# One branch around the whole second layer of a two-layer transformer kernel, six PSUM banks in turn in its feed-forward part, and gathers and modulations issued at other places

## The reference

```python
# attention: 16 heads, 64 anchors
anchor_B = qk @ W_anchor.T * SCALE
attn = softmax(anchor_B, axis=-1)
s = sum(attn, axis=-2); recip = 1 / s
out = einsum('bhna,bhnd->bhad', attn, v)
out = recip[..., None] * out
out = einsum('bhna,bhad->bhnd', attn, out)
out = out @ W_out.T + b_out
# feed-forward: width 512
h = silu(x @ w1.T * s1) * (x @ w2.T * s2)
h = gelu(h @ h1.T * sh1); h = gelu(h @ h2.T * sh2)
y = h @ w3.T * s3
# around both: layernorm, times (1 + c), plus s; result times a gate, plus x
```

## Time and profile before

| | |
|---|---|
| median of 3 runs | 864.3 us (861.33 to 867.69) |
| the profiled execution: its time / its span | 871.6 us / 869.8 us |
| busy share: PE, DVE, ACT, POOL | 80%, 64%, 48%, 32% |
| mean granted clock of PE | 0.885 of full |
| the chain that ended last: PE, DVE, POOL, issue, DMA, ACT | 53%, 16%, 13%, 8%, 4%, 4% |
| first tile's sum of batches 0, 1, 2, 3 starts at (L553) | 380.36, 505.33, 628.88, 752.17 us |

### The profile page before, as it was taken

The page is one execution under the profiler, slowest core; times in us unless marked ns, Lnnn a source line. Parts: engine busy times, 40 slices in busy tenths (PEclk is TensorE's granted clock), DMA queues, the critical chain, the costliest instruction groups (busy, mean ns, idle before and its releaser), DMA issues.

```text
span 869.8 us, 9514 instructions
## 1 busy us (share of the span) xinstructions
PE 700.2 (80%) x3009; PEld 498.2 (57%) x3009; DVE 559.6 (64%) x1355; ACT 416.9 (48%) x701; POOL 279.9 (32%) x222
## 2 busy tenths in 40 slices
PE   3676555379999992099888989979898989899997
PEld 1665444358888881055546845546655458555465
DVE  4585554747677671558487579586586875676563
ACT  2455332257777770134337534347444265343474
POOL 2347787600000003627531047430058230043000
PEclk8788755579999997569899999999999999799999
DMA  5244337727677661000000000000000000000000
GB/s 202 109 146 172 140 123 271 274 61 252 237 236 266 228 211 61 24 1 24 25 0 1 1 32 25 19 2 0 26 16 26 9 1 1 26 1 1 0 1 26
DMA packets 21554, 71.22 MB, mean 82 GB/s; under 512 B 4908, under 2 KB 5172, under 8 KB 17080
## 3 DMA queue, kind: packets, MB, share of 16 engines
q1 hardware_dynamic: 17400, 62.08, 20.3%
q0 software_dynamic: 4096, 8.40, 3.2%
HBM read 47.38 MB, written 23.08 MB: 81 GB/s over the span
## 4 chain that ended last, share of the span: by engine, by line
PE 53%; DVE 16%; POOL 13%; issue 8%; DMA 4%; ACT 4%; another core or an unknown queue 1%; SPq 0%; DVEq 0%; ACTq 0%; POOLq 0%
PE ps L1389 13%; PE ps L1385 7%; PE ps L1391 7%; POOL rows_by_expert L498 7%; PE ps L1393 6%; PE ps L1392 6%; PE ps L1645 5%; POOL yb L525 3%; DVE hid L1283 2%; PE ps L1633 2%; DMA wbuf<-w_split 2%; DVE stats L894 2%; PE ps L1661 2%; DVE ring L1299 2%; POOL misc L563 2%
## 5 line engine op out<-in xcount | busy, mean ns | idle before, releaser
L525 POOL DMA_INDIRECT yb<-y_by_expert,ypos x64 | 64.0, 1000 | 184.2 <-DMA y_by_expert<-ysb 168.0
L1389 PE MATMUL ps<-hid,fh 128*128 128x512 f32 x256 | 103.6, 405 | 6.6 <-DVE hid L1283 4.9
L1391 PE MATMUL ps<-hid,fh 128*128 128x512 f32 x256 | 100.3, 392 | 0.0
L563 POOL TENSOR_TENSOR misc<-misc,ring 128x1024 f32<-128x1024 f32 x28 | 65.9, 2354 | 51.6 <-DVE ring L1273 38.1
L498 POOL DMA_INDIRECT rows_by_expert<-h,pos x64 | 68.4, 1069 | 23.1 <-issue 19.8
L1283 DVE TENSOR_TENSOR hid<-ring,hid 128x512 fp32r<-128x512 f32 x56 | 45.1, 810 | 46.5 <-ACT hid L794 45.2
L1389 PEld LDWEIGHTS ps<-hid,fh 128*128 128x128 f32 x256 | 48.1, 188 | 25.9 <-DVE hid L1283 11.3
L1645 PE MATMUL ps<-ring,hn 128*128 128x512 f32 x112 | 55.5, 618 | 5.3 <-DVE ring L1273 5.3
L1177 DVE TENSOR_TENSOR hid<-ring,hid 128x512 fp32r<-128x512 f32 x46 | 31.8, 692 | 41.9 <-ACT hid L590 41.9
L1661 PE MATMUL ps<-attnT,cmat 128*128 128x512 f32 x128 | 56.9, 592 | 0.0
L1252 DVE TENSOR_REDUCE nmax<-ps 128x16 f32<-128x1024 f32 x32 | 39.2, 1224 | 25.5 <-PE ps L1393 25.5
(11 more groups left out here) (278 smaller groups left out, 1744.8 us busy)
## 6 DMA issues: line engine op xcount, KB each, us to landing
wbuf<-w_split SPq DMA_DIRECT2D x23, 1024.0 KB, 5.3
w_split<-parts SPq DMA_DIRECT2D x4, 2048.0 KB, 7.6
xs<-rows_by_expert SPq DMA_DIRECT2D x23, 256.0 KB, 5.3
y_by_expert<-ysb SPq DMA_DIRECT2D x23, 256.0 KB, 5.6
raw<-in_w SPq DMA_DIRECT2D x8, 512.0 KB, 8.4
ffn_raw<-in_ffn SPq DMA_DIRECT2D x1, 2816.0 KB
rows_by_expert<-zeros SPq DMA_DIRECT2D x9, 256.0 KB, 8.2
xa<-in_x SPq DMA_DIRECT2D x4, 512.0 KB, 6.0
```

The lines of the kernel that those rows point to most:

```text
L525: gp.indirect_dma_start(yb[:, k, t, :], None, ydisp, bass.IndirectOffsetOnAxis(ypos[:, b, k, t:t + 1].bitcast(U32), 0))\
L563: gp.tensor_tensor(asum, asum, ring[:, 2 * (t % 2):2 * (t % 2) + 2, :] .rearrange("p a n -> p (a n)"), ALU.add).then_inc(*pool_asum.raise_(t))
L1389: te.matmul(out_, w(0), x(0), start=first, stop=False)
L1391: return te.matmul(out_, w(0), x(1), start=False, stop=last_)
```

## The change

The branch now stands once, around the whole second layer, `second_layer(all_)`: PE's code of the attention is there in both forms too. The outputs of the feed-forward part, y included, go round six banks, 2 to 7. On POOL the first pair of gathers is issued ahead of the first running sum, and no pair stands between the sixth and the seventh sum. The modulations of batch b+1 wait until DVE has written the last remainder of (1,ab). DVE takes `residual("A", 0)` ahead of `normalized("L1a", 0)`, and `normalized("L1a", 1)` goes behind `normalized("L1b", 0)`. PE makes the logits of tile 1 and transposes the maxima of tile 0 ahead of y of group 1, and shifts behind it; ACT copies these maxima ahead of y's copy.

```diff
+        ffn_outs = [j for o in ffn_order for j in ffn_jobs(*o)]
+        FFN_BANKS = 6
+        def ffn_bank(*job):
+            return 2 + (ffn_outs.index(job) + 1) % FFN_BANKS
...
@@ POOL: attention of batch b
+                if more:
+                    gather(b + 1, places[0:2])
                 for t in range(1, T):
                     pool.wait_ge(*dve_attn.now(t, b))
...
                     gp.tensor_tensor(asum, asum, ring[:, 2 * (t % 2):2 * (t % 2) + 2, :]
                                      .rearrange("p a n -> p (a n)"), ALU.add).then_inc(*pool_asum.raise_(t))
-                    if more:
-                        gather(b + 1, places[2 * t - 2:2 * t] if t < T - 1 else places[2 * t - 2:])
+                    if more and t < T - 2:
+                        gather(b + 1, places[2 * t:2 * t + 2])
+                if more:
+                    gather(b + 1, places[2 * (T - 2):])
...
                 if more:
+                    pool.wait_ge(*dve_split.now((1, "ab", HC - 1), b))
                     for g in gs2:
                         modulate(g, b + 1)
...
@@ ACT
+            maxT_out(0, 0)
             for b in bs:
...
-                    if t < T:
-                        act.wait_ge(*pe_maxT.now(t, b))
-                        if t >= 1:
-                            act.wait_ge(*pe_shift.now(t - 1, b))
-                        copy(mTs[:, :], ps[0:32, 1, 0:128]).then_inc(*act_maxT.raise_(t))
+                    if 0 < t < T:
+                        maxT_out(t, b)
...
                     load_table(ACT.Exp)
+                    maxT_out(0, b + 1)
                 out_y(1, b)
@@ DVE
                     for g in gs2:
                         combine(b + 1, g)
-                    normalized("L1a", 0, b + 1)
                 residual("A", 0, 1, b)
                 if more:
+                    normalized("L1a", 0, b + 1)
+                normalized("L1b", 0, b)
+                if more:
                     normalized("L1a", 1, b + 1)
-                normalized("L1b", 0, b)
                 hT_ffn(0, b)
@@ PE
             def bank_read(job, b):
                 i = ffn_outs.index(job)
-                if i < 4:
+                if i < FFN_BANKS:
                     return act_y.now(("A", 1), b)
...
-                residual_transposed("F", 0, Y_BANK[0], b)
+                residual_transposed("F", 0, ffn_bank(0, "y"), b)
                 if more:
                     logits(0, b + 1)
+                    logits(1, b + 1)
+                    max_transposed(0, b + 1)
                 last_layer(1, b, all_)
                 if more:
-                    logits(1, b + 1)
-                    max_transposed(0, b + 1)
                     shift(0, b + 1)
-                residual_transposed("F", 1, Y_BANK[1], b)
+                residual_transposed("F", 1, ffn_bank(1, "y"), b)
...
-                with pe.If_eq(inexact, 0):
-                    ffn(b, more, False)
-                for ev, n in before.items():
-                    ev.raised = n
-                with pe.Else():
-                    ffn(b, more, True)
...
+            with pe.If_eq(inexact, 0):
+                second_layer(False)
+            for ev, n in before.items():
+                ev.raised = n
+            with pe.Else():
+                second_layer(True)
```

More of the change, by code:

```diff
@@ L809, in _, with maxT_out @@
                 hT_attn(0, g)
+            def maxT_out(t, b):
+                act.wait_ge(*pe_maxT.now(t, b))
+                if t >= 1:
+                    act.wait_ge(*pe_shift.now(t - 1, b))
+                copy(mTs[:, :], ps[0:32, 1, 0:128]).then_inc(*act_maxT.raise_(t))
             load_table(ACT.Exp)
+            maxT_out(0, 0)
             for b in bs:
@@ L1372, in _ @@
                 hidden(1, "h2", b)
-                residual("F", 0, Y_BANK[0], b)
+                residual("F", 0, ffn_bank(0, "y"), b)
                 if more:
@@ L1376, in _ @@
                     neg_max(1, b + 1)
-                residual("F", 1, Y_BANK[1], b)
+                residual("F", 1, ffn_bank(1, "y"), b)
         @block.tensor
@@ L1679, in bank_read @@
                 i = ffn_outs.index(job)
[L1680 removed]
+                if i < FFN_BANKS:
                     return act_y.now(("A", 1), b)
[L1682 removed]
+                g, part, *c = ffn_outs[i - FFN_BANKS]
                 if part == "b":
[L1684 to L1688 removed]
+                    return dve_prod.now((g, *c), b)
+                return act_ffn.now((g, "ab" if part == "a" else part, *c), b)
             def first_layer(g, b, all_):
@@ L1709, in hidden_layer @@
                             at_ = kc * 512 + o * 128
-                            last_ = three(ps[:, ffn_bank((g, part, o)), :], lambda i: w[:, i, at_:at_ + 128],
+                            last_ = three(ps[:, ffn_bank(g, part, o), :], lambda i: w[:, i, at_:at_ + 128],
                                           lambda i: x[:, kc, i, :], kc == 0, kc == HC - 1, all_)
@@ L1716, in last_layer @@
                 x = hset(sets[g, "h2"])
-                pe.wait_ge(*act_zs.now("z", b))
+                pe.wait_ge(*bank_read((g, "y"), b))
                 for kc in cs:
                     pe.wait_ge(*dve_split.now((g, "h2", kc), b))
-                    last_ = three(ps[:, Y_BANK[g], :], lambda i: fy[:, i, kc * 128:(kc + 1) * 128],
+                    last_ = three(ps[:, ffn_bank(g, "y"), :], lambda i: fy[:, i, kc * 128:(kc + 1) * 128],
                                   lambda i: x[:, kc, i, :], kc == 0, kc == HC - 1, all_)
@@ new lines, in ffn, with second_layer @@
+                residual_transposed("F", 1, ffn_bank(1, "y"), b)
+            def second_layer(all_):
+                h2_transposed(0, 0)
+                h2_transposed(1, 0)
+                logits(0, 0)
+                logits(1, 0)
+                max_transposed(0, 0)
+                shift(0, 0)
+                for b in bs:
+                    more = b + 1 < B
+                    for t in range(T + 2):
+                        if t >= 2:
+                            gather(t - 2, b)
+                        if 0 < t < T:
+                            max_transposed(t, b)
+                        if t >= 2:
+                            attn_transposed(t - 2, b)
+                        if 2 <= t + 1 < T:
+                            logits(t + 1, b)
+                        if 0 < t < T:
+                            shift(t, b)
+                    pe.wait_ge(*pool_asum.now(T - 1, b))
+                    asum = misc[:, :, :].rearrange("p a n -> p (a n)")
+                    for k in range(AC):
+                        last = te.matmul(ps[:, 5, k:k + 1], asum[:, k * 128:(k + 1) * 128], ones[:, :], start=True, stop=True)
+                    last.then_inc(*pe_fin.raise_("s"))
+                    pe.wait_ge(*act_zs.now("z", b))
+                    zT = ring[:, 0:2, :].rearrange("p a n -> p (a n)")
+                    for j in range(4):
+                        if j == 3:
+                            pe.wait_ge(*dve_srec.now("s", b))
+                        for k in range(2):
+                            q = 2 * j + k
+                            last = te.matmul(ps[:, 2 + j, k * 256:(k + 1) * 256], zT[:, q * 128:(q + 1) * 128],
+                                             vout[:, q * 256:(q + 1) * 256], start=True, stop=True)
+                        last.then_inc(*pe_fin.raise_(("C", j)))
+                    pe.wait_ge(*act_attnT.now((T - 1, 1), b))
+                    outputs(0, range(AC), b)
+                    outputs(1, range(1), b)
+                    residual_transposed("A", 0, 1, b)
+                    outputs(1, range(1, 7), b)
+                    h3_transposed(0, b)
+                    outputs(1, range(7, AC), b)
+                    residual_transposed("A", 1, 1, b)
+                    ffn(b, more, all_)
@@ L1801 @@
+            before = {ev: ev.raised for ev in every}
+            with pe.If_eq(inexact, 0):
[4 more added lines that the diff above has]
+                second_layer(True)
 def kernel(**inputs):
```

64 lines of the change are left out of this document (7 added, 57 removed).

## The result

The changed kernel takes 838.9 us (median of four runs, 837.56 to 840.78); the kernel before, with one more run, 865.8. The ratio is 0.969, 95% interval 0.965 to 0.973. The forecast was 835.6 us with a range of 829 to 848. The profiled execution took 839.1 us, with a span of 837.3. All ratios are of fast executions alone; the profiled ones of e5 and e8 were slower (856.4 and 885.5 us), and only distances and clocks inside them are read.

The account below looks back on a forecast made before the run. In the feed-forward part PE was taken to bound only from the second gated layer on, ACT and DVE before that. Gains 15.5 + 5.8 + 5.9 + 0 + 1.5 = 28.7 off the 864.3 median gave 835.6 us, range 829 to 848.

Parts of the forecast that it names:

- End of the attention: Last scaled tile to residual, batches 0 to 2: earlier last sum and DVE's new order make it 17.24, gaining 15.5 us.
- The 6.25 for batch 0: Batch 0's share of the 15.5 us gain at the end of the attention, from 23.49 between tile and residual.
- Modulations: Gated layers, batches 0 to 2: first product to Gelu falls from 8.85 to 6.91, gaining 3 x 1.94 = 5.8 us.
- Six banks: Second output chunk of (0,h2) starts 1.47 earlier in all four batches, gaining 5.9 us.
- From batch to batch: Removed jump (2.07) offset by a new wait: 0 for batches 1 and 2, 1.5 us gained in batch 3.
- the wait ahead of y: Handover between batches: PE stands still 1.8 us for the maxima of tile 0 before it makes y.
- Rival 1: Clock falls in the new wait ahead of y, slowing y and the starts of batches 1 and 2: 848.5 us, chance 0.17.
- Rivals 2, 3 and 4: Late modulated rows, 845.4, 0.13; first tiles at 1.2 GHz, 869.8, 0.04; late gathers and larger branch body, 858.5, 0.04.

Follow-up runs that it names:

- e5: Changed kernel with the old order from batch to batch, ACT's copy of the maxima again behind y's copy: 842.1 us, ratio 0.960 to the kernel before.
- e8: Kernel before plus six matmuls nobody reads, in every batch, while PE waits for the last sum: 874.1 us, ratio 0.995.
- e1: Kernel before with the new order of gathers alone: 855.0 us against 867.2, ratio 0.987.
- e7: Kernel before with DVE's new order of normalizations and residual alone: 876.3 us against 878.6, ratio 0.998.
- e10: Kernel before plus nine matmuls nobody reads while PE waits for the last sum, batches 0 to 2 only: 861.6 us against 868.5, ratio 0.993.
- e2: Kernel before with the modulations alone moved behind the last remainder of (1,ab): 861.7 us against 867.2, ratio 0.993.
- r2: Changed kernel with the old order from batch to batch, run again beside the changed kernel (838.2 us): 833.5 us, ratio 0.959 to the kernel before.
- e3: Kernel before with six banks alone: 862.0 us against 867.2, ratio 0.994.
- e6: Kernel before with the new order from batch to batch alone, ACT's copy of the maxima ahead of y's copy: 885.0 us against 878.6, ratio 1.009.
- e4: Kernel before with one branch around the second layer alone, old order from batch to batch: 862.8 us against 867.2, ratio 0.993.
- e9: Changed kernel with the old order of gathers, two again between the last two sums: 853.1 us, ratio 0.985 to the kernel before.

## Why the prediction was right, step by step

*End of the attention*: forecast 15.5, found 15.0. The step holds as it was worked out, wait and clock. e1 gives 11.3 for the gathers alone and e7's trace 1.02 a batch for the normalization, for which the forecast took 1.14; that is most of why the residual is at 17.40 and not at 17.24. That the two gathers are free in their new place is shown by e1. Of the 15.0, the wait has 3 x 1.75 = 5.3 (4.50 to 2.75), the clock 1.7 + 1.7 + 3.3 = 6.7, the normalization 3.1; e10 gets its 6.1 us from the clock alone, without moving a transfer. The 6.25 for batch 0 was a reading of one trace, in which the clock happened to stay low longer there; with that wait it was so in nine batches of 21.

*Modulations*: forecast 5.8, found 5.8 in the trace and 5.9 in e2. DVE and POOL taking turns was read rightly, as an exclusive lock (the Trainium skill's page "SBUF — State Buffer", section "SBUF: two separate sides", names it so); at the new place it costs DVE as much as before, on work that nobody waits for: Gelu to POOL's product is 43.6 with the modulations there (r2) and 43.5 without them (e3).

*Six banks*: forecast 1.47 a batch, found 1.40 (e3) and 1.35 in batch 3.

*From batch to batch*: the wait ahead of y was forecast at 1.8 and is 1.60; POOL's first product comes 1.6 later by the forecast, and 1.58 by e6. Removing the jump alone gains 5.6 us (e4); in the change that is largely used up by the new wait. The Trainium skill's rule on taken branches ("Runtime: NRT & Kernel Launch", "Instruction fetch mechanics") agrees with this stall, though no run here shows that it is a fetch. The term of the sum that was mis-sized is this one: 0 for batches 1 and 2 and 1.5 for batch 3. From Gelu to the last tile of the next batch the traces gain 0.25, 1.67 and 2.91 with the banks' share in them, 4.8; forecast were 5.9. So batch 1 gave less than forecast, as the clock fell in the changed kernel's first product there and had not before; batch 3 gave what was forecast. One trace is a weak ground for this term, though. From POOL's first product to the last tile, in batches 1 to 3, it took 36.7 to 40.9 in the 21 batches with the jump and the old order (mean 39.2), 35.9 to 37.5 in the nine with one branch and that order (36.4), and 35.9 to 37.6 in the nine with one branch and the new order (37.2). By these means the change's net is 3 x 2.0, less the 4.8 ahead of POOL's product: 1.2, for 1.5 in the forecast.

*What the profiled execution had too much of*: batch 0's attention is 1.58 shorter after, though in neither kernel a jump or the new wait lies ahead of it. In the other traces it takes 35.9 to 37.9, whatever the kernel (e2 35.92, e4 37.86), and what differs here is the clock at its start. PE's first product takes 3.78 in the kernel before and 1.98 in the changed one; in the midst of it, before and after (columns as above):

```profile
384.00:386.00 2.00, 2.00 (x4) 0.51 (x3) 1.93 (x3) 0.00 (x0) 0.00 (x0) 0.50 0.00 0
...
378.00:380.00 2.00, 2.00 (x6) 0.92 (x7) 1.93 (x4) 1.02 (x1) 1.53 (x3) 1.00 0.00 0
```

The sum had no term for this 1.58, and without it the rows give 27.0. I had subtracted 28.7 from the median, yet it was worked out from an execution that stood 7.3 above it. So that the total comes as near as 28.5 is in part luck; what parts 28.5 from 26.8 was not tested by itself.

*Rival 1* (the clock falls in the new waits) was right in part. It did not fall on y in any batch, but on PE's first product in batches 1 and 3, behind the wait of 1.45 for POOL. Batch 2 had the same wait and kept 2.4 GHz, in both traces of the changed kernel. Clock in batch 1 of the changed kernel:

```profile
492.00:494.00 2.00, 0.55 (x3) 0.11 (x2) 1.93 (x3) 1.02 (x1) 1.90 (x1) 1.00 0.05 16
494.00:496.00 2.00, 2.00 (x3) 0.96 (x4) 1.93 (x4) 0.00 (x0) 1.61 (x2) 0.51 0.10 29
```

The first product then takes twice as long and the attention 37.6 in place of 35.9: 1.7 us each time. *Rivals 2, 3 and 4* did not come: the modulated rows are just in time, no batch stayed at 1.2 GHz beyond its first tile's product, and the combination is never late (quotients to residual 8.21 in batches 0 to 2, as in e7, which moved no gather).

The parts sum up within their errors. Alone they gain 11.3, 5.9, 5.0, 5.6 and 2.2 us, 30.0, and the order from batch to batch loses 7.5: 22.5 for all, with an uncertainty of some 9 when the six intervals are put together. The change, reckoned the same way, gains 26.5 and, on the second occasion, 30.7. Whether it gains more than its parts these runs can't tell.

## What to carry to other kernels

Where a kernel holds an instance of a stage without the work that overlaps it in the others, such as a last iteration, set the two side by side by distances: the difference is what the overlapped work costs, clock included. Where the clock is part of it, do so in more than one trace. Put work that nobody waits for behind what another engine waits for in the same queue, and modulations of POOL where DVE's products are not on the path. Before moving a step ahead of a dense piece on PE, ask when its input is ready: here the transposition of maxima that DVE was still making held back y by 1.6 us, three times. Whether the logits of tile 1 alone could go ahead of y without loss was not run.

## What the hardware showed

A wait of 1.60 us ahead of 16 one-column matmuls was enough to bring the value products behind them to 1.2 GHz for much of their length (mean granted clock over them 0.54 to 0.71) in every batch that had it (21 of 21: batches 0 to 2 of the kernel before and of e2, e3, e4, e6, e7 and e9), and the quotients came 1.7 or 3.3 us later for it beyond the wait itself (12.63 and 14.28 less 4.50, against 9.19 less 2.75); where the wait is gone they were never late (15 of 15 in e1, e5, r2 and the two traces of the change). Nine matmuls that nobody reads bought back 6.1 us (3.6 to 8.6). A taken jump over the long form of a feed-forward part cost PE 2.07 to 2.57 us in the kernel before and 2.05 to 3.05 over all eight kernels that have it. The test that falls through, at the start of the feed-forward part, costs nothing that shows: residual to first gated product is 9.77 or 9.78 in batches 0 to 2 with it (before) and without it (after).
